# Transformer block on one core: weights' high and low parts kept in DRAM by the first batch and loaded by the others; half the output projection inside attention

## The reference

```python
mod = (_silu(L0_c) @ L0_wmod).reshape(L0_c.shape[0], 6, 1, -1)
sa, ca, ga, sb, cb, gb = (mod[:, 0], mod[:, 1], mod[:, 2], mod[:, 3], mod[:, 4], mod[:, 5])
ga = (2 * (ga >= 0) - 1) * jnp.maximum(jnp.abs(ga), 0.25)
gb = (2 * (gb >= 0) - 1) * jnp.maximum(jnp.abs(gb), 0.25)
h = _layernorm(x, axis=-1) * (1 + ca) + sa
x = x + ga * _L0_attn_ref(h, L0_attn_wq, L0_attn_wk, L0_attn_wv, L0_attn_wo)
h = _layernorm(x, axis=-1) * (1 + cb) + sb
x = x + gb * _L0_ffn_ref(h, L0_ffn_gate_w, L0_ffn_lora_A, L0_ffn_lora_B)
```

## Time and profile before

| what | value |
|---|---|
| median of three runs | 2837.13 us |
| the profiled execution: time, span | 2837.69 us, 2835.9 us |
| busy: TensorE, DVE, ACT, POOL | 2665.6, 1822.5, 1384.9, 882.4 us |
| granted TensorE clock, mean | 0.982 |
| DMA moved | 273 MB, mean 96 GB/s |
| an ordinary group | 76.0 us |

### The profile page before, as it was taken

One profiled execution on the slowest core, in us unless ns is written; L12 is line 12 of the kernel. 1 busy time (PEld: TensorE's weight loads), 2 busy tenths in 40 slices (PEclk: granted clock), 3 DMA queues, 4 the chain that ended last, 5 costly groups with the idle time before them and its releaser, 6 DMA issues.

```text
span 2835.9 us, 41435 instructions
## 1 busy us (share of the span) xinstructions
PE 2665.6 (94%) x12889; PEld 2159.1 (76%) x12889; DVE 1822.5 (64%) x4131; ACT 1384.9 (49%) x2822; POOL 882.4 (31%) x380
## 2 busy tenths in 40 slices
PE   5799999999899999999899999999899999998999
PEld 3478777777787787777778877877777778776777
DVE  3366666665866666667776666667766676667543
ACT  3255555554455555444455554444454454445341
POOL 2133333322333333332333333333323233333112
PEclk8799999999999999999999999999999999999999
DMA  7622222213333222224223332124222222224211
GB/s 271 223 93 86 89 89 75 67 64 137 111 97 96 90 88 67 69 72 141 98 89 96 96 96 71 63 72 158 90 74 67 73 82 75 74 80 158 90 74 53
DMA packets 169589, 273.21 MB, mean 96 GB/s; under 512 B 8272, under 2 KB 99728, under 8 KB 168208
## 3 DMA queue, kind: packets, MB, share of 16 engines
q1 hardware_dynamic: 164240, 253.05, 27.1%
q10 hardware_dynamic: 5248, 18.91, 1.8%
HBM read 242.54 MB, written 29.39 MB: 96 GB/s over the span
## 4 chain that ended last, share of the span: by engine, by line
PE 54%; DVE 22%; issue 9%; ACT 7%; DMA 1%; ACTq 1%; DVEq 1%; SPq 0%
PE bank L527 17%; PE bank L528 17%; PE bank L529 17%; DVE rotated L849 8%; DVE swapped L846 4%; DVE prob L878 3%; DVE prob L888 3%; ACT swapped L697 2%; PE bank L584 2%; ACT swapped L696 1%; DVE qo_lo L870 1%; ACT w_o_hi L474 1%; ACT prob L713 1%; ACT pT_hi L768 1%; DMA hT_lo<-hT_lo_scratch 1%
## 5 line engine op out<-in xcount | busy, mean ns | idle before, releaser
L479 POOL TENSOR_TENSOR w_o_lo<-stage,w_o_hi 128x1024 fp32r<-128x1024 f32 x128 | 308.7, 2412 | 533.2 <-ACT w_o_hi L474 533.2
L527 PE MATMUL bank<-w_o_hi,qo_hi 128*128 128x512 f32 x1024 | 400.2, 391 | 4.4 <-DVE acc L865 4.4
L527 PE MATMUL bank<-hT_hi,w_q_hi 128*128 128x512 f32 x1024 | 400.5, 391 | 0.5 <-DVE swapped L846 0.2
L528 PE MATMUL bank<-hT_lo,w_q_hi 128*128 128x512 f32 x1024 | 399.2, 390 | 0.0
L529 PE MATMUL bank<-hT_hi,w_q_lo 128*128 128x512 f32 x1024 | 398.9, 390 | 0.0
L529 PE MATMUL bank<-w_o_hi,qo_lo 128*128 128x512 f32 x1024 | 398.5, 389 | 0.0
L528 PE MATMUL bank<-w_o_lo,qo_hi 128*128 128x512 f32 x1024 | 398.5, 389 | 0.0
L479 POOL TENSOR_TENSOR w_q_lo<-stage,w_q_hi 128x1024 fp32r<-128x1024 f32 x128 | 313.6, 2458 | 189.6 <-ACT w_q_hi L474 189.6
L479 POOL TENSOR_TENSOR w_v_lo<-stage,w_v_hi 128x1024 fp32r<-128x1024 f32 x32 | 76.8, 2399 | 933.8 <-ACT w_v_hi L474 933.8
L713 ACT ACTIVATE prob<-prob,nbias 128x384 f32<-128x384 f32 (+2 forms) x512 | 273.7, 535 | 157.5 <-DVE nbias L878 143.6
L865 DVE TENSOR_TENSOR acc<-bank,acc 128x512 f32<-128x512 f32 x256 | 171.7, 687 | 235.7 <-PE bank L529 235.7
(11 more groups left out here) (188 smaller groups left out, 5621.6 us busy)
## 6 DMA issues: line engine op xcount, KB each, us to landing
stage<-in_wq SPq DMA_DIRECT2D x128, 512.0 KB, 3.6
stage<-in_wo SPq DMA_DIRECT2D x128, 512.0 KB, 3.3
stage<-in_wk SPq DMA_DIRECT2D x33, 512.0 KB, 3.6
stage<-in_wv SPq DMA_DIRECT2D x32, 512.0 KB, 3.6
acc<-in_wmod SPq DMA_DIRECT2D x32, 512.0 KB, 5.9
xb<-in_x ACTq DMA_DIRECT2D x20, 512.0 KB, 5.3
wm<-in_wmod SPq DMA_DIRECT2D x8, 1024.0 KB, 12.0
x1s<-x_scratch SPq DMA_DIRECT2D x4, 2048.0 KB, 8.8
```

The costliest lines, as they stand in the source:

```text
L479: eng.tensor_tensor(dst[1], src, dst[0].bitcast(F32), ALU.subtract).then_inc(s_split, 1)
L527: eng.matmul(o, st[0], mv_[0], start=start, stop=False)
L528: eng.matmul(o, st[0], mv_[1], start=False, stop=False)
```

## The change

Batch 0 splits as before, and after each chunk SP stores both parts in a DRAM scratch (sp_keep). In batches 1 to 3 SP loads the parts straight into the weight tiles (sp_fetch, sp_direct_group); ACT's copies and POOL's subtractions fall away, and POOL does nothing there but clear acc. The low part of the layer-norm tile goes from POOL to DVE (dve_tile_lo), and pe_tile to between Q0 and Q1. From the attention of group 7 on, four of the eight halves of the output projection stand inside attention, behind units 8, 10, 12 and 14 (WO_AT), all in bank 1, and DVE adds them at its steps 12, 14, 16 and 18. Outputs have bank 7 alone, and values 2 move from the end to unit 13, in batch 0 too. K's products stand at units 0 to 7. At the end, the second layer norm's first chain runs inside the last attention, and in the next quarters' statistics one product (dve_us) goes between the second and the third.

```diff
+FILL = 4
...
+    w_d = {kind: [nc.dram_tensor(f"w_{kind}_{z}_scratch", (KV * P, cols), F32, kind="Internal").ap() for z in ("hi", "lo")]
+           for kind, cols in (("v", KT * HD), ("k", KT * HD), ("q", KT * GQ * HD), ("o", GQ * D))}
...
+        def sp_keep(eng, j, g):
+
+            for z in range(2):
+                eng.dma_start(kept(j, z, g), flat(j, z)).then_inc(s_ws[j], 16)
+
+        def sp_fetch(eng, j, g, landed):
+
+            for z in range(2):
+                eng.dma_start(flat(j, z), kept(j, z, g)).then_inc(landed, 16)
...
+        def sp_direct_group(eng, n, before_o=None):
+
+            eng.wait_ge(s_proj, 6 * n + 1)
+            for j in range(1, 5):
+                sp_fetch(eng, j, n % KV, s_dq[j - 1])
+            sp_fetch(eng, 0, n % KV, s_dv)
+            eng.wait_ge(s_proj, 6 * n + 2)
+            sp_fetch(eng, 5, (n + 1) % KV, s_dk)
+            if before_o:
+                before_o()
+            eng.wait_ge(s_wo, 8 * n + 1)
+            for j in range(6, NC):
+                sp_fetch(eng, j, n % KV, s_do)
...
+        def p1_sp(eng):
+            last = BATCH - 1
...
+            with eng.Fori(1 + QT, KV) as n:
                 for j in range(NC):
...
                     sp_chunk(eng, n, j)
+                    jj, nn = (NC - 2 + j, n - 1) if j < 2 else (j - 2, n)
+                    sp_keep(eng, jj, (nn + 1) % KV if jj == 5 else nn)
...
+            sp_reload(eng, 1)
+            for j in range(NC):
+                eng.wait_ge(s_ws[j], 32 * KV)
+            sp_direct_group(eng, KV)
...
+            with eng.Fori(1, BATCH) as b:
                 eng.wait_ge(s_fin, 2 * QT * b)
-            plain(eng.memset(acc[:], 0.0)).then_inc(s_acc0, 1)
...
+                plain(eng.memset(acc[:], 0.0)).then_inc(s_acc0, 1)
...
-        def pe_wo(eng, n, half):
+        def wo_bank(half, fill):
+
+            return bank[1] if fill and half < FILL else SBANK[half % 3]
+
+        def pe_wo(eng, n, half, fill, direct):
...
             if c == 0:
                 eng.wait_ge(s_ol, QT * n + t + 1)
-            if half >= 3:
+            if fill and 1 <= half < FILL:
+                eng.wait_ge(s_wor, 8 * n + half + 1)
+            elif half >= (FILL + 3 if fill else 3):
                 eng.wait_ge(s_wor, 8 * n + half - 1)
...
-        OBANK = [bank[7], bank[1]]
+        OBANK = bank[7]
...
-            elif i >= 2:
-                eng.wait_ge(s_ol, QT * n + i - 1)
+            else:
+                eng.wait_ge(s_ol, QT * n + i)
...
-        K_AT = (0, 1, 2, 3, 5, 7, 12, 13)
-
-        K_LAST = (4, 5, 7, 8, 10, 11, 13, 14)
-
-        def pe_attention(eng, n, k_at, b1=None):
+        K_AT = (0, 1, 2, 3, 4, 5, 6, 7)
+        K_SPLIT = (0, 1, 2, 3, 5, 7, 12, 13)
+
+        K_LAST = (3, 4, 5, 6, 7, 9, 11, 13)
+        WO_AT = (8, 10, 12, 14)
+
+        def pe_attention(eng, n, k_at, fill, k_direct, b1=None, o_direct=True):
...
-                if u % GQ == 1 and GQ < u < UNITS - GQ:
+                if u % GQ == 1 and u > GQ:
                     pe_values(eng, n, u // GQ - 1)
-            for i in (QT - 2, QT - 1):
-                pe_values(eng, n, i)
-
-        def pe_qv(eng, n):
+                if fill and u in WO_AT:
+                    pe_wo(eng, n, WO_AT.index(u), True, o_direct)
+            pe_values(eng, n, QT - 1)
...
-        OUT_STEP = {GQ * i + GQ + 1 + LAG: i for i in range(QT - 2)}
...
+        OUT_STEP = {GQ * i + GQ + 1 + LAG: i for i in range(QT - 1)}
...
+                if fill and s - 4 in WO_AT:
+                    if s - 4 == WO_AT[0]:
+                        eng.wait_ge(s_acc0, b + 1)
+                    dve_wo(eng, n, WO_AT.index(s - 4))
+            dve_outputs(eng, n, QT - 1)
...
+        def act_last(eng, s):
+
+            if s == 9:
+                act_sqrt2(eng, 0)
+            if 12 <= s < 12 + QT:
+                act_normalise2(eng, 0, (s - 12,))
+            if s in (16, 17):
+                eng.wait_ge(u_a, 16)
+                act_a_hi(eng, s - 16)
...
+                        if i == 1:
+                            dve_us(eng, t, 1)
```

More of the change, by code:

```diff
@@ L412, in sp_groups, with sp_reload @@
+        def sp_reload(eng, b1):
+            n = b1 * KV
+            eng.wait_ge(s_proj, 6 * n + 1)
+            eng.wait_ge(s_hst, 32 * QT * b1)
+            for q in range(KT // 2):
+                for z in range(2):
+                    eng.dma_start(hT[z][:, 2 * q:2 * q + 2, :].bitcast(F32), hT_d[z][bass.ds(b1 * P, P), 2 * q:2 * q + 2, :]).then_inc(s_hl[q], 16)
         def sp_groups(eng, b, rows, store):
             for t in range(QT):
-                n, i = b * KV + 1 + t, b * QT + t
+                n = b * KV + 1 + t
+                sp_direct_group(eng, n, lambda: sp_tile_load(eng, n, rows(t)))
+                if store:
+                    sp_tile_store(eng, b, t)
+            with eng.Fori(1 + QT, KV) as g:
+                sp_direct_group(eng, b * KV + g)
@@ L705, in act_rope @@
             eng.activation(dst, rotated[slot][:], ACT.Copy).then_inc(s_rh, 1)
[L706 removed]
+            if split and r == GQ - 1:
                 act_chunk(eng, n, NC - 1)
@@ L727, in act_project @@
             if tile is not None:
-                act_tile(eng, tile)
+                act_tile(eng, tile, range(KT))
             for r in range(1, 1 + GQ):
-                act_rope(eng, n, r)
+                act_rope(eng, n, r, True)
+            if tile is not None:
+                eng.wait_ge(s_hst, 32 * (tile + 1))
+        def act_project(eng, n, batch_done=None, tile=None):
+            act_rope(eng, n, 0, False)
+            if tile is not None:
+                act_tile_sqrt(eng, tile)
+            for r in range(1, 1 + GQ):
+                act_rope(eng, n, r, False)
+                if r <= 2 and tile is not None:
+                    act_tile(eng, tile, range(4 * (r - 1), 4 * r))
                 if r == 2 and batch_done is not None:
@@ L1014, in dve_groups @@
                     dve_tile2(eng, g)
-                    dve_wo(eng, n - 1, 3)
-                for half in range(4, 8):
+                    dve_wo(eng, n - 1, 6)
+                dve_wo(eng, n - 1, 7)
+                for r in range(1, 1 + GQ):
+                    if ln and r == 3:
+                        dve_tile_lo(eng, i)
+                    dve_rope(eng, n, r)
+            with eng.Fori(1 + QT, KV) as g:
+                n = b * KV + g
+                dve_attention(eng, n - 1, b)
+                dve_rope(eng, n, 0)
+                for half in range(FILL, 8):
                     dve_wo(eng, n - 1, half)
@@ L1321, in p2_dve @@
             res = lambda t: dve_residual(eng, BATCH - 1, t, BATCH + 1)
-            dve_chain2(eng, 0, lambda: dve_wo(eng, LAST, 0))
-            for half in range(1, 4):
-                dve_wo(eng, LAST, half)
-            res(0)
             for half in range(4, 8):
```

362 lines of the change are left out of this document (216 added, 146 removed).

## The result

The changed kernel takes 2823.97 us (median of 4 runs, 2821.13 to 2825.52) against 2839.24 us before (4 runs, the three from above among them): ratio 0.9944, interval 0.9926 to 0.9961, 15 us or 0.5% faster. The forecast was 2807, 31 us or 1.1% faster, in a range of 2778 to 2834. The direction came, and a little under half of the size. The profiled execution took 2825.5 us with a span of 2823.7, against 2835.9.

What follows compares the result with a forecast made beforehand. TensorE's own matmuls were taken to set the end, so only its idle time could be won. Terms +3 - 13 - 23 + 0 + 7 - 5 = -31 us from 2837.7 gave 2806.7, stated as 2807 us; range 2778 to 2834.

Steps and rivals of the forecast that it cites:

- Part 1: Half the output projection inside 21 attentions: wins 2.85 us, gives back 3.1, +0.15 each, +3 us in all.
- Part 2: No splitting in batches 1 to 3: first transpose no longer waits, -0.6 us for 22 groups, -13 us.
- Part 4: Attention at a batch's end (groups 7, 15, 23), K waiting for the hT reload: about 0 us, bounds -6 and +8.
- Part 3: Groups after a batch's end (8, 16, 24): no Q, V or first transpose waits, -23 us, bounds -24 and -12.
- Part 5: Batch 0's seven attentions, values 2 at unit 13 and one shared bank: +7 us, bounds 0 and +10.
- rule against it: Skill's warning that frequent small idles swing the clock; attention's 1.5 us waits were still taken at full clock.
- stores cost nothing: Batch 0: 80 MB of stores beside the loads; w_q's chunk 4 has 6.5 us of slack, so nothing lost.
- Rival (d): Batch 0's stores hold up the chunk loads, 3.5 us over the slack, 25 us in all: 2832; chance 0.08.
- Part 6: The end: last gate matmul 1 us earlier, -4 at the 5.16 us wait for DVE; -5 us, bounds -12 and 0.
- Rival (a): 21 attentions: clock falls behind the fill's waits, +55 or +109 us, so 2862 to 2916; chance 0.08.
- (b): 21 attentions: the fill's waits are half as long because DVE gets ahead, -1.5 us each, 2775; chance 0.1.
- (c): Batch ends: residuals late again, TensorE waits as before, loses 12 to 20 of the 23 us: 2819 to 2827; chance 0.12.

Runs made afterwards that it cites:

- e4: e1's edit, plus no output projection inside the attentions of the first seven groups of batches 1 to 3, against the changed kernel: 2803.9 us.
- e5: DVE adds each half of the fill at the start of its step instead of the end, against the changed kernel: 2783.0 us.
- e6: Half 3 of the fill moved from unit 14 to behind the transposes of unit 15, against the changed kernel: 2786.8 us.
- e9: POOL's memset of acc waits for DVE's last rotation in the group after a batch's end, against the changed kernel: 2826.5 us.
- e1: Groups 0 to 6 get back the second output bank and the old order of values 2 and 3, against the changed kernel: 2809.1 us.
- e13: Last two K triples moved from units 12 and 13 to behind the transposes of 14 and 15 in batch 0, against the changed kernel: 2812.9 us.
- e10: ACT's square root moved ahead of the split of w_q's second chunk in batch 0's tile groups, against the changed kernel: 2817.3 us.
- e3: Only group 0's weight parts stored, batches 1 to 3 loading those same parts for every group, against the changed kernel: 2813.4 us.
- e14: Each store of batch 0 issued twice, the second into an unread scratch, against the changed kernel: 2941.4 us.
- e7: The last batch's four residuals moved out of the stretch between half 6 and the gate, against the changed kernel: 2816.2 us.

## Why the prediction was half right

**Part 1, the fill: right.** Both waits came at their places with 1.5 and 1.4 us of lost issue time, attention 36.2 for 36.4. The term of +0.15 should have been +0.3 (e4), because without splitting the unfilled attention also gets 0.2 shorter. What the prediction did not draw from its own timetable: both waits hang on nothing but order, and e5 and e6 remove them with a few lines each. The fill then wins 2.8 us an attention against e4 instead of losing 0.3.

**Part 2: right**, -0.6 a group. **Part 4:** -3.6 for 0, inside its bounds; K still waited for the reload (3.1 us at 698.93 in group 7, 4.1 at the longest). **Part 3: the sum right, its lower bound wrong.** -25.8 for -24.4. The bound of -12 held that the memset's share was half of it. A memset laid on the same two rows (e9) costs 5 us over the three groups (2.5 by the medians), not 12 to 18: it lets TensorE wait only by as much as DVE is late already. By exclusion, most of the 23 us was DVE's backlog beside POOL's splitting; no run gave POOL its splitting back, so this is argued and not shown, and so is how the backlog divides into ropes and residuals.

**Part 5 failed: +20.6 for +7.** The step "share one bank" had its wait right and left out the clock: 26.5 us an attention at full clock (26.4 forecast), but in four of seven the clock fell to the 1.2 GHz level behind it, some 5 us by those attentions' lengths; group 0's lower clock at its head adds 1.3. e1 and e13 took away the wait and the falls with it. I had weighed the clock for waits of 1.5 us in batches 1 to 3 and not for the longer one that my own times gave for batch 0 (T15 issued by 21.85, last values at 24.35: 2.5 us of lost issue time, 2.06 of it recorded as idle). The "rule against it" took 3.56 us as the shortest wait with a fall behind it., shown above it, have a shorter one: 1.86 us at 679.13, in a window at clock 0.76. Read with that row, a wait of over 2 us had to be given a price. The step "stores cost nothing" looked at one consumer of the late loads, w_q's last chunk with 6.5 us of slack. That one held; the load of the chunk ahead of it held up ACT, and with it the square root of the tile: 6.7 us, of which e10 took back 4 and e3 nearly all. A delay must be followed down the queue of every engine that waits for it. Rival (d) named the right traffic and the wrong victim; at twice the dose the right one fell too (e14).

**Part 6 failed: +4.1 for -5.6** (+0.6 to +4.1 over the runs with this code). Of the 4 us at the 5.16 us wait 1.2 came. The step "the last gate matmul comes 1 us earlier" did not place the four residuals in DVE's list: counted from group 31's first Q that matmul comes 1.8 us later, behind 2.4 us more of waits and a lower clock. Two of the residuals moved from beside the output projection to the stretch in front of the gate; e7, which moves them on, wins 7.8 (4 to 8 by the stretch alone).

**Rival (a)**, the clock behind the fill's waits, did not come where I put it: windows of ordinary groups show 1.00, with two waits of 1.2 us recorded in each attention. Rivals (b) and (c) did not come either: the waits had their forecast length, and groups 8, 16 and 24 gained 25.8. The rule weighed in the prediction (the Trainium skill, page "TensorE: Matmul & The Clock Gate", section "A second HAM failure mode: psum-queue depth-cycling", on frequent small idles between groups of matmuls) is not borne out at that length; one bank too few did cost clock where it made a wait of 2.06 us.

## What to carry to other kernels

A fill takes a covered wait's cover away as easily as it fills one: write the consumers' order on the other engine together with it, place adds that free a bank at the head of their step, and keep one filler for the last chain. A delay is priced at all engines that wait for it in order, and extra traffic beside a stage whose loads are waited for had a cliff here, so slack at one consumer is no licence. Where a kernel gets a second variant of a loop, that variant needs its own timetable: here batch 0 and the tail lost over half of what the rest had won, two thirds by the profile.
